# Fewer slots between the steps of a feed-forward tile in a hand-timed attention schedule

## The reference

```python
cq = rms_norm(x @ w_qa.T); q = cq @ w_qb.T            # 16 heads of 128 + 64 (rotated)
ckv = x @ w_kva.T; kv = rms_norm(ckv[:, :128]) @ w_kvb.T
scores = (q_full @ k_full.T) * scale, causal mask, softmax
x = layernorm(x + (attn @ v) @ w_o.T)
x = layernorm(x + x @ (weight * scale_weight).T + bias)
```

## Time and profile before

| | us |
|---|---|
| median of 3 runs | 1728.51 |
| lowest and highest | 1726.79 and 1729.55 |
| the profiled execution, its own time | 1728.51 |
| its span in the profile | 1726.6 |
| PE, DVE, ACT, POOL busy | 1681.6, 1380.9, 1122.5, 979.1 |
| granted TensorE clock, mean | 0.997 |

### The profile page before, as it was taken

The page is one execution under the profiler, slowest core; times in us unless marked ns, Lnnn a source line. Parts: engine busy times, 40 slices in busy tenths (PEclk is TensorE's granted clock), DMA queues, the critical chain, the costliest instruction groups (busy, mean ns, idle before and its releaser), DMA issues.

```text
span 1726.6 us, 28510 instructions
## 1 busy us (share of the span) xinstructions
PE 1681.6 (97%) x8789; PEld 1397.3 (81%) x8789; DVE 1380.9 (80%) x2498; ACT 1122.5 (65%) x2128; POOL 979.1 (57%) x932
## 2 busy tenths in 40 slices
PE   7998999999999999999999999999999999999997
PEld 5566788888888888888888888888888888888775
DVE  3555788888888897878888888888888888888984
ACT  3554666676667676666667666766666777676774
POOL 4322555565565565555566555656556655656785
PEclk9999999999999999999999999999999999999999
DMA  6996321212321322223211412123222111111322
GB/s 189 360 341 236 109 87 43 80 52 90 128 66 57 111 68 77 71 66 131 80 56 50 135 51 79 48 85 112 68 74 103 57 53 65 50 43 44 135 92 80
DMA packets 113246, 169.27 MB, mean 98 GB/s; under 512 B 13648, under 2 KB 84304, under 8 KB 110800
## 3 DMA queue, kind: packets, MB, share of 16 engines
q1 hardware_dynamic: 105936, 125.08, 22.4%
q10 hardware_dynamic: 2304, 26.22, 3.8%
q0 software_dynamic: 4864, 16.26, 2.8%
HBM read 101.98 MB, written 65.54 MB: 97 GB/s over the span
## 4 chain that ended last, share of the span: by engine, by line
PE 88%; POOL 4%; DMA 3%; DVE 3%; issue 2%; ACT 1%; DVEq 0%; SPq 0%; ACTq 0%; POOLq 0%
PE rows L1456 35%; PE bank L1486 7%; PE bank L1489 7%; PE bank L1487 7%; PE rows L1519 7%; PE rows L1419 5%; PE bank L1519 3%; PE rows L1432 2%; PE bank L1419 2%; PE rows L388 2%; DMA cq_dram<-cq 2%; PE bank L1476 2%; PE bank L1432 1%; POOL split_p L1714 1%; PE rows L1465 1%
## 5 line engine op out<-in xcount | busy, mean ns | idle before, releaser
L1714 POOL TENSOR_TENSOR split_p<-pool,split_p 128x512 fp32r<-128x512 f32 x544 | 703.1, 1294 | 503.4 <-ACT split_p L1605 503.1
L1456 PE MATMUL rows<-q_c,key_c 128*128 128x512 f32 x1632 | 477.5, 401 | 1.4 <-DVE top L1830 1.4
L1593 ACT COPY pool<-rows 128x512 f32<-128x512 f32 x480 | 281.8, 587 | 232.0 <-PE rows L1456 231.2
L1830 DVE TENSOR_TENSOR top<-rows,top 128x512 f32<-128x512 f32 x420 | 288.6, 687 | 124.7 <-ACT pool L1593 121.2
L1845 DVE TENSOR_TENSOR pool<-bank,pool 128x512 f32<-128x512 f32 x544 | 369.6, 679 | 19.8 <-PE bank L1476 19.8
L1598 ACT ACTIVATE pool<-pool 128x512 f32<-128x512 f32 x544 | 346.0, 636 | 18.0 <-DVE pool L1845 17.1
L1605 ACT CAST split_p<-pool 128x512 fp32r<-128x512 f32 x544 | 333.2, 613 | 17.0 <-PE bank L1489 16.7
L1456 PE MATMUL rows<-q_pe,key_pe 128*128 128x512 f32 x1088 | 337.9, 392 | 4.0 <-DMA q_pe<-pe_dram 4.0
L1857 DVE TENSOR_TENSOR bank<-bank,pool 128x512 f32<-128x512 f32 x480 | 330.9, 689 | 0.0
L1456 PEld LDWEIGHTS rows<-q_c,key_c 128*128 128x128 f32 x1632 | 288.5, 189 | 50.2 <-DVE top L1830 5.1
L1456 PEld LDWEIGHTS rows<-q_pe,key_pe 128*128 128x128 f32 x1088 | 204.6, 188 | 50.0 <-DMA q_pe<-pe_dram 4.5
(11 more groups left out here) (191 smaller groups left out, 2136.6 us busy)
## 6 DMA issues: line engine op xcount, KB each, us to landing
q_pe<-pe_dram SPq DMA_DIRECT2D x128, 128.0 KB, 2.6
y_dram<-y SPq DMA_DIRECT2D x62, 256.0 KB, 2.0
cq<-cq_dram SPq DMA_DIRECT2D x20, 768.0 KB, 4.8
y<-y_dram SPq DMA_DIRECT2D x48, 256.0 KB, 3.0
wq_dram<-wq ACTq DMA_DIRECT2D x4, 2304.0 KB, 10.0
wo_dram<-wo ACTq DMA_DIRECT2D x4, 2048.0 KB, 8.9
pe_dram<-by_sin SPq DMA_DIRECT2D x32, 256.0 KB, 2.1
pe_dram<-by_cos SPq DMA_DIRECT2D x32, 256.0 KB, 2.2
```

What stands on the lines that cost most here:

```text
L1456: mm = pe.matmul(by_head(out), k, q, start=(z == 0), stop=(z == 4))
L1593: nc.scalar.copy(slot(n), SCORES[n % N_SCORES]).then_inc(scores_copied, 1)
L1714: nc.gpsimd.tensor_tensor(split_p[:, n % 2, 1, :], slot(n), stored(split_p[:, n % 2, 0, :]), ALU.subtract).then_inc(p_lo, 1)
L1830: nc.vector.tensor_tensor(out, SCORES[n % N_SCORES], slot(number(it, 0)) if t == 1 else out, ALU.max).then_inc(scores_maxed, 1)
```

## The change

The first slot of the feed-forward tiles becomes one earlier (W_SLOT + 5 in place of + 6), and the distances between the steps of a tile become shorter. FFN_SLOT was 543, 545, ... 567, 570, 572, 574 and is 542, 544, ... 564, 567, 570, 572, 574. Relative to score tiles, for the tiles up to 11, linear u comes two slots earlier, z_statistics two, z_invert, apply and out three (for tiles 12 to 15 one less, their slots being the same). centre u and invert u move to phase SPREAD, ahead of the exp, hi and lo of their slot. No instruction is added or removed, and nothing ahead of slot 538 or so is touched.

```diff
-        slots.append(max(slots[-1] + PACE if slots else W_SLOT + 6, ready))
+        slots.append(max(slots[-1] + PACE if slots else W_SLOT + 5, ready))
...
         if u < DIRECT:
-            yield n - 3, FFN, ("in", u)
-        yield n + 0, SPREAD, ("statistics", u)
-        yield n + 0, ROUND, ("centre", u)
-        yield n + 1, FFN, ("invert", u)
+            yield n - 4, FFN, ("in", u)
+        yield n, SPREAD, ("statistics", u)
+        yield n, SPREAD, ("centre", u)
+        yield n, SPREAD, ("invert", u)
         yield n + 1, FFN_TURN, ("turn", u)
-        yield n + 2, FFN, ("scale", u)
-        yield n + 3, FFN, ("add_bias", u)
-        yield n + 4, FFN_LINEAR, ("linear", u)
-        yield n + 5, MAX, ("z_statistics", u)
-        yield n + 6, READ, ("z_invert", u)
-        yield n + 8, COPIES, ("apply", u)
-        yield n + 8, COPIES, ("out", u)
+        yield n + 1, FFN, ("scale", u)
+        yield n + 1, FFN, ("add_bias", u)
+        yield n + 3, FFN_LINEAR, ("linear", u)
+        yield n + 4, FFN, ("z_statistics", u)
+        yield n + 4, FFN, ("z_invert", u)
+        yield n + 6, FFN, ("apply", u)
+        yield n + 6, FFN, ("out", u)
```

## The result

The changed kernel takes 1739.21 us (median of 4 runs, 1738.63 to 1740.15), the kernel before, timed with it, 1728.67 (1726.79 to 1729.55, 4 runs). The ratio is 1.006 with a 95% interval of 1.0048 to 1.0073: slower, by 10.5 us. The forecast was 1732.0 with a range up to 1737.5, so the result lies outside it. The direction was right: it had the largest chance of the three (47 in 100). Its size was not.

What follows compares the result with a forecast made beforehand. PE (97% busy) bounds the kernel, POOL paces the middle. Losses of 0.8, 0.5 and 0.7 plus 5.9 moved work make 8.0; the tail returns 5.3; +2.7, with 0.9 added +3.6: 1732.0 us, range 1727 to 1737.5.

Steps and rivals of the forecast that it cites:

- Part 1: The start, up to lo 528: late x_in 0 stalls DVE and ACT; lo 528 6.7 us later, 0.8 lost.
- Part 2: The middle, lo 528 to lo 538: z_invert's wait about covered; 0.5 us of waits over five periods.
- the way: From lo 528's end through linear 2 and z_statistics to z_invert 2: 6.1 us, against POOL's own 6.11.
- The rival of the longer loop: Middle: the way takes 6.6 us, not 6.1, so z_invert waits every period; +5, 1737; 18 in 100.
- The rival of the clock: Hole on PE from 1611.5 and a few behind it: clock falls, costing 2.5 us; 1735; 5 in 100.
- Part 3: From lo 538 to values 543: z_invert 7 and linear 8 wait; 23.4 us against 22.7, 0.7 lost.
- the walk: Carrying the new queues forward from the profile rows, each step starting when its engine and inputs are ready.
- the 0.9: Microseconds added for linear 7, 9, 12 and 13, counted as 2.8 us to z where the rows say 3.04.
- Part 4: From values 543 to the end: 17.6 us to y 63, then 23.7; the tail 5.3 us shorter.
- the correction: The 0.9 us added for linears counted too short; half set behind y 63, giving 24.2 there.

Runs made afterwards that it cites:

- e6: Changed kernel with x_in of tiles 0 to 3 loaded ahead of the feed-forward weights: 1736.76 us.
- e16: Changed kernel with the first slot as before (W_SLOT + 6) and centre back in phase ROUND: 1731.07 us, ratio 1.0036.
- e11: Changed kernel with centre alone back in phase ROUND, behind exp and hi: 1735.83 us, ratio 1.0056.
- e5: Changed kernel with the whole z group (z_invert, apply, out) back at its old distances: 1738.34 us.
- e1: Changed kernel with the first slot put back (W_SLOT + 6), short distances kept: 1733.97 us, ratio 1.0048.
- e8: The changed kernel again without edit, on a second chip with a second trace: 1739.60 us.
- e13: Changed kernel with x_in of tiles 0 to 3 loaded ahead of the weights, centre back and the z group back: 1733.70 us, ratio 1.0046.
- e12: Kernel before with only centre and invert moved to slot n, phase SPREAD: 1749.10 us, ratio 1.0129.
- e2: Changed kernel with z_invert alone put back to slot n + 6, phase READ: 1754.01 us, ratio 1.0166.
- e3: Changed kernel with centre back in phase ROUND and invert back in slot n + 1, phase FFN: 1761.33 us, ratio 1.0209.
- e15: Kernel before with the shorter distances for tiles 12 to 15 alone: 1729.65 us.

## Why the prediction was wrong

**Part 1, the start, was right in its mechanism.** Forecast and measured: statistics 0 waits 2.3 and 2.70 us, centre 0 4.5 and 5.22, lo 522 is 4.4 and 4.96 later, lo 528 6.7 and 7.6 (6.7 in the second execution). The rule that the prediction took from the Trainium skill (TensorE: Matmul & The Clock Gate, section "Architectural detail: the array is 16× 32×32, not 1× 128×128"), first in, first out, is borne out: exp 523 did not pass centre 0. The loss was put too low: e6 removes the load's wait and wins 2.8 us (2.0 to 2.7 by the ruler), where I had called only 0.8 of the delay lost. The fall of the clock there, which e6 has not, may be part of that price; the two were not parted.

**Part 2, the middle, is the step that failed.** "So the way is just covered: the wait is nothing or a few tenths", 0.5 us over five periods. Measured: 35.4 against 30.5 us, so 4.9, all of it at three z_inverts (1.57, 0.18 and 3.18). In a plain period the sum was right: z_invert 1 and z_invert 2 start 6.1 us apart, at 1630.68 and 1636.76. But the way was walked as one row of steps of one tile, and the changes of iteration put others in it: a spread_max behind linear 3 on PE, with the whole of DVE behind it, and copy_out behind centre 6 on ACT. I had named "ACT has slack too: centre u waits for statistics u, and hi comes 1.2 us ahead of its lo" as the cover; the waits of statistics (2.69) and of DVE for spread_max (2.35 and 3.15) are each about twice those 1.2 or more. I treated ACT and DVE as each having slack of its own, and did not see that the chain closes to a ring, so that a wait on one comes back on the other. That order and place of the steps make the loss is shown: of the 7.4 us from lo 528 to values 543, 2.5 are there with the shorter distances alone (e16), 4.8 with the earlier slot too (e11), and all with centre ahead as well; z_invert's distance is a small part (1.9, e5). That a ring carries it is read from the waits of the traces; e11 loosens one link of it, centre, and wins 2.6 of the 7.4.

**The rival of the longer loop** gave 1737 and had 18 in 100. Its sign was right and its mechanism half: it wanted z_invert to wait in every period, but POOL waits at eleven of sixteen, up to 3.4 us, and e5 shows that taking these waits away wins little. Its +5 us is close to the 4.9 of part 2, but not for its reason: the plain periods have no such wait, and the two long ones stand where the iteration changes.

**The rival of the clock** had 5 in 100 and came true three times in the same kernel. Its price, 2.5 us a fall, was too high: e16 against e1, e11 and the changed kernel puts the fall at linear 13 at about 1.6 us. Linear 5 took 3.98 (4.58 in e8) and not 3.00, and PE's busy time is 4.3 us more in all, 6.4 in e8. It also misread the trace: before, PE's last matmul ends at 1717.86 and the clock falls at about 1721.6, so some 3.7 us later and not 2. Its chance was far too low: I foresaw a hole at the start and one of 2.9 us in the tail, and priced a single fall.

**Part 3** was +0.7 by the walk, +1.2 with its share of the 0.9, and is +2.5 (25.1 against 22.6). With the slot back it is 23.8 (e1) and 23.7 (e16), as forecast, and e11 leaves it at 24.3; which wait it is was not followed.

**Part 4, the tail,** was −5.3. To y 63 it is right: 18.3 against 17.6 forecast. From y 63 to the end I forecast 23.7, 24.2 with the correction, and it took 26.4; before it took 25.7. The hole was foreseen well (2.9 against 3.00), as were its causes, statistics 14 behind z 12 and z_statistics 12. Its fall of the clock was not: without it, in e16, this stretch takes 24.8, so the fall is 1.6 of the 2.2 us between forecast and result, and of the other 0.6 I can show no cause.

In sum, from lo 521: forecast +3.6, measured +13.0 (12.3 in the second execution). The 9.4 between them are 0.9 in the start, 4.3 in the middle, 1.3 up to values 543, 0.7 up to y 63 and 2.2 behind it.

**Still open.** The parts do not add up: alone e6, e11 and e5 win 2.8, 3.4 to 3.8 and 1.3, but together 5.5 to 5.9. e13 shows why in one place (the fall of the clock at linear 0), and no more than that. The falls at the start and in the middle have no price of their own. Why centre ahead, with invert, costs 20.9 us in the middle with the old distances (e12), and centre only 0.2 with the short ones and the later slot (e1 against e16), was not followed. And the 0.36% of e16 were not taken apart into invert, scale, add_bias, linear and the z group.

## What to carry to other kernels

Where several engines work through fixed queues, the place of a waiting step matters more than its own time: ahead of the step that feeds the bound engine, its wait is everybody's (e12: no work added, 22 us, falls of the clock included). But a place has no fixed price: take the parts of a change away in pairs, and not only one by one (e1, e11 and e16). Check a new order not only in the plain period but where the pattern breaks, here at each change of iteration, and follow the chain until it closes; slack on two engines of one ring must not be counted twice. When steps of one tile are moved, move those that wait for them too, or they wait at once (e2 and e3).

## What was unexpected in the hardware

The granted clock fell to 0.50 behind holes of PE of 2.27, 1.99 and 3.00 us in the changed kernel, and at the same three places in a second execution, there behind 1.36, 1.99 and 3.00. Yet with a hole of 1.87 in e6, of 1.99 in e5, of 2.21 and 3.00 in e16 and of 3.00 in e15 it stayed at 1.00, and in e5 it fell at 1660.7 behind holes of 1.04 and 0.63. So the length of one hole doesn't tell it. The Trainium skill (TensorE: Matmul & The Clock Gate, section "Why this matters for your kernels") warns of gaps between bursts; the three falls agree, but e15 and e16 show gaps without a fall.

One such fall, at linear 13, cost about 1.6 us of time (e16 against e1, e11 and the changed kernel).
